# A recurrence between expert units: the x terms of four steps in one batch, the state product moved, VectorE's unit pass split over two gaps

## The reference

```python
logits = concatenate([x, h]) @ W_attn.T + b_attn        # 64 values
applied = softmax(logits) @ enc                          # enc: 64 x 128 of this sample
comb = relu(concatenate([x, applied]) @ W_comb.T + b_comb)
h = tanh(comb @ W_ih.T + b_ih + h @ W_hh.T + b_hh)
out = h @ W_out.T + b_out                                # 0 once a step with mean(x) == 0 came
```

## Time and profile before

| | us |
|---|---|
| Median of 3 runs | 1224.45 |
| Lowest, highest | 1223.15, 1224.51 |
| Profiled execution, its own time | 1223.28 |
| Its span, first to last instruction | 1221.2 |
| PE busy in the span | 1055.8 (86%) |
| DVE, POOL, ACT busy | 742.1, 512.8, 429.8 |
| Mean granted TensorE clock, share of 2.4 GHz | 0.864 |

### The profile page before, as it was taken

How to read it: one execution, slowest core, us unless ns; L and a number is a source line. 1 busy time by engine, 2 the same in 40 slices (tenths; PEclk the granted TensorE clock), 3 DMA queues, 4 the chain that set the end, 5 groups by cost and what they waited for, 6 DMA issues and landing times. The chain is left out here.

```text
span 1221.2 us, 31046 instructions
## 1 busy us (share of the span) xinstructions
PE 1055.8 (86%) x12668; PEld 701.2 (57%) x12668; DVE 742.1 (61%) x1882; ACT 429.8 (35%) x798; POOL 512.8 (42%) x452
## 2 busy tenths in 40 slices
PE   2699777789998999989997997799899999997867
PEld 2577655545555555545553443677677677775445
DVE  5544444445567554765569565678777678775553
ACT  1211011112221221212221222677778677775111
POOL 4788200003322332322333455576666666664010
PEclk9555555559999998889999999799999999999878
DMA  9020026012212221113222342000000000000000
GB/s 241 19 57 1 1 43 121 1 47 63 70 53 54 74 70 54 53 36 74 70 70 70 90 121 70 1 3 3 3 3 2 3 3 3 2 3 3 1 18 17
DMA packets 46066, 51.67 MB, mean 42 GB/s; under 512 B 22086, under 2 KB 36584, under 8 KB 45928
## 3 DMA queue, kind: packets, MB, share of 16 engines
q1 hardware_dynamic: 43010, 48.71, 15.7%
q10 hardware_dynamic: 2918, 1.01, 0.5%
HBM read 48.13 MB, written 1.57 MB: 41 GB/s over the span
## 5 line engine op out<-in xcount | busy, mean ns | idle before, releaser
L637 POOL TENSOR_TENSOR ex<-ex,xn 128x512 f32<-128x512 f32 x128 | 162.5, 1271 | 368.0 <-DVE ex L1173 275.3
L801 ACT ACTIVATE thcb<-ps 128x512 f32<-128x512 f32 x132 | 78.6, 596 | 283.1 <-PE ps L1529 283.1
L702 POOL TENSOR_TENSOR wu<-encC,wu 128x1024 f16<-128x1024 f32 x64 | 137.7, 2167 | 56.5 <-ACT encC L876 56.5
L1168 DVE SCALAR_TENSOR_TENSOR ex<-thcb,ps 128x512 f32<-128x512 f32 x132 | 90.6, 687 | 89.8 <-ACT thcb L801 87.1
L1536 PE MATMUL ps<-ex,wd 128*128 128x512 f32 x256 | 138.9, 625 | 1.9 <-POOL ex L637 1.9
L1529 PE MATMUL ps<-xnT,wg 128*128 (+1 forms) x384 | 109.3, 395 | 6.5 <-DVE ex L1173 6.4
L1529 PE MATMUL ps<-xnT,wu 128*128 (+1 forms) x384 | 109.7, 396 | 0.0
L1589 PE MATMUL ps<-wg,M 128*128 128x128 f16 x1536 | 98.2, 222 | 2.1 <-DVE wg L1262 2.1
L1589 PEld LDWEIGHTS ps<-wg,M 128*128 128x128 f16 x1536 | 93.1, 99 | 6.8 <-DVE wg L1262 2.5
L1173 DVE TENSOR_TENSOR ex<-ex,ps 128x512 f32<-128x512 f32 x132 | 90.7, 687 | 7.3 <-POOL ex L637 2.8
L696 POOL TENSOR_TENSOR wd<-wd,a_sum 128x512 f32<-128x512 f32 x64 | 66.5, 1042 | 65.7 <-DVE a_sum L1293 65.7
(11 more groups left out here) (295 smaller groups left out, 1937.1 us busy)
## 6 DMA issues: line engine op xcount, KB each, us to landing
xn<-coef_rows SPq DMA_DIRECT2D x128, 256.0 KB, 3.8
thcb<-in_L_ffn_Wg SPq DMA_DIRECT2D x8, 256.0 KB, 3.8
thcb<-in_L_ffn_Wu SPq DMA_DIRECT2D x8, 256.0 KB, 3.1
wd<-in_L_ffn_Wd SPq DMA_DIRECT2D x2, 1024.0 KB, 11.4
xtok<-in_x SPq DMA_DIRECT2D x4, 256.0 KB, 6.0
thcb<-in_ctx SPq DMA_DIRECT2D x2, 512.0 KB, 11.1
wu<-in_L_xcond_attn_wq SPq DMA_DIRECT2D x2, 512.0 KB, 10.9
wu<-in_L_xcond_attn_wk SPq DMA_DIRECT2D x2, 512.0 KB, 10.6
```

The source lines that it names most:

```text
L637: nc.gpsimd.tensor_tensor(hid[:, n % 2, :], gu[:, n % 2, :], other, ALU.mult)\
L702: nc.gpsimd.tensor_tensor(z[:, 1, 8 * u:8 * u + 8, :], a_Zc[:, u], z[:, 0, 8 * u:8 * u + 8, :], ALU.subtract)\
L801: nc.scalar.activation(th[:, n % 2, :], bank(n % 2), ACT.Tanh, scale=0.5 / WSCALE)\
L1168: V.scalar_tensor_tensor(ga[:, :], th[:, n % 2, :], 1.0, bank(n % 2), add, mul)\
```

## The change

Six things.

- The recurrence has two banks in every stage, 6 and 4. Bank 6 (`X_BANK`) holds, for four steps at once, comb (128 columns, 32 for each step) and the logits (partitions 32 times the step's number in its four); bank 4 (`Y_BANK`) the transposed exp and `hn`. `e_sb`, `nmax`, `esum`, `rsum` and `diag` use the same 32 partitions as the step's logits.
- `x_parts`: W_comb's x part, the logits' x part and the bias row of four steps, three matmuls of 128 columns, behind `hn` of every fourth step (and ahead of the first). The step itself has none of them. `xnc` and its copy are gone.
- The W_hh product comes right behind the 48 in every stage, and the 48 begin on the high half of `eb` alone.
- VectorE's unit is split: `gated` (first pass) one gap after TensorE's, `product` (second pass) two gaps after, ahead of all but the recurrence in its gap.
- Sides alternate over all units (`side`), also from chunk to chunk, and everything waits for the unit before the last. The shared unit has a gap of its own, one later; `END_GAP` goes from 96 to 97 and with it the sum into xT to gap 33.
- The loop over stages 2 and 3 is written out.

```diff
@@ -153,11 +152,11 @@
...
-        e_sb = sb("e_sb", [B, 2 * L])
-        nmax = sb("nmax", [B, 1])
-        esum = sb("esum", [B, 1])
-        rsum = sb("rsum", [B, 1])
-        diag = sb("diag", [B, B])
+        e_sb = sb("e_sb", [P, 2 * L])
+        nmax = sb("nmax", [P, 1])
+        esum = sb("esum", [P, 1])
+        rsum = sb("rsum", [P, 1])
+        diag = sb("diag", [P, B])
         eb = sb("eb", [P, 2, B], F16)
@@ -310,16 +309,19 @@
...
-        def step_banks(k):
-            return (7, 6, 5, 4) if first(k) else (6, 6, 6, 6)
+        X_BANK, Y_BANK = 6, 4
...
-        COMB, ET, HN = (slice(2 * L + i * B, 2 * L + (i + 1) * B) for i in range(3))
+        ET, HN = slice(0, B), slice(B, 2 * B)
+        LOGITS = slice(TL * B, TL * B + 2 * L)
+        def rows(st):
+            return slice(st % TL * B, (st % TL + 1) * B)
@@ -437,7 +439,7 @@
...
         U0 = 28
-        unit_gap = [U0 + 2 * min(n, PAIRS - 1) for n in range(UNITS)]
+        unit_gap = [U0 + 2 * n - (n == PAIRS) for n in range(UNITS)]
         END_GAP = unit_gap[-1] + 6
@@ -447,17 +449,19 @@
...
-            if isinstance(m, int) and m == 0 and n < 2:
-                return None
-            return m * UNITS + n - (1 if n else 0)
+            done = m * UNITS + n
+            return done - 1 if done >= 2 else None
+        def side(m, n):
+            return (m * UNITS + n) % 2
...
             stage(1, 0, None, True)
-            with eng.Fori(0, CH - 2) as j:
-                stage(j + 2, j + 1, j, True)
+            for k in range(2, CH):
+                stage(k, k - 1, k - 2, True)
             stage(CH, CH - 1, CH - 2, False)
@@ -634,7 +638,7 @@
...
                 other = wide if n < PAIRS else k_shared.broadcast_to([P, CT])
-                nc.gpsimd.tensor_tensor(hid[:, n % 2, :], gu[:, n % 2, :], other, ALU.mult)\
+                nc.gpsimd.tensor_tensor(hid[:, side(m, n), :], gu[:, side(m, n), :], other, ALU.mult)\
                   .then_inc(s["hid_ready"], 1)
@@ -762,20 +766,15 @@
...
                 act.wait_ge(s["nmax_ready"], t + 1)
-                nc.scalar.activation(e_sb[:, :], bank(step_banks(k)[0])[0:B, 0:2 * L], ACT.Exp, bias=nmax[:, :],
-                                     accum_out=esum[:, :]).then_inc(s["exp_ready"], 1)
+                r = rows(st)
+                nc.scalar.activation(e_sb[r, :], bank(X_BANK)[r, LOGITS], ACT.Exp, bias=nmax[r, :],
+                                     accum_out=esum[r, :]).then_inc(s["exp_ready"], 1)
...
                 act.wait_ge(s["hn_ready"], t + 1)
-                nc.scalar.activation(Hc[:, st, :], bank(step_banks(k)[3])[:, HN], ACT.Tanh, bias=bh[:, :])\
+                nc.scalar.activation(Hc[:, st, :], bank(Y_BANK)[:, HN], ACT.Tanh, bias=bh[:, :])\
                   .then_inc(s["h_ready"], 1)
-            def xn_chunk(k):
-                if not first(k):
-                    act.wait_ge(s["hn_ready"], k * SPC)
-                nc.scalar.copy(xnc[:, :], xnT[:, bass.ds(k * CT, CT)]).then_inc(s["xnc_ready"], 1)
@@ -798,12 +797,10 @@
...
                     act.wait_ge(s["gu_ready"], others(m, n))
-                nc.scalar.activation(th[:, n % 2, :], bank(n % 2), ACT.Tanh, scale=0.5 / WSCALE)\
+                nc.scalar.activation(th[:, side(m, n), :], bank(side(m, n)), ACT.Tanh, scale=0.5 / WSCALE)\
                   .then_inc(s["th_ready"], 1)
             def stage(k, m, tail, recur):
-                if recur:
-                    xn_chunk(k)
                 for gap in gaps_of(m, tail):
@@ -1014,28 +1011,28 @@
...
                 t = k * SPC + st
-                logits_bank, comb_bank, eT_bank, _ = (bank(i) for i in step_banks(k))
+                x_bank, eT, r = bank(X_BANK), bank(Y_BANK)[:, ET], rows(st)
                 if place == 0:
                     dve.wait_ge(s["logits_ready"], t + 1)
-                    V.tensor_reduce(nmax[:, :], logits_bank[0:B, 0:L], AX_X, ALU.max, negate=True)\
+                    V.tensor_reduce(nmax[r, :], x_bank[r, LOGITS.start:LOGITS.start + L], AX_X, ALU.max, negate=True)\
                      .then_inc(s["nmax_ready"], 1)
...
                     dve.wait_ge(s["exp_ready"], t + 1)
-                    rt.settle(V.reciprocal(rsum[:, :], esum[:, :]))
-                    V.tensor_scalar(diag[:, :], ident[0:B, 0:B], rsum[:, :], 2.0, mul, mul)\
+                    rt.settle(V.reciprocal(rsum[r, :], esum[r, :]))
+                    V.tensor_scalar(diag[r, :], ident[r, r], rsum[r, :], 2.0, mul, mul)\
                      .then_inc(s["diag_ready"], 1)
...
-                    V.tensor_tensor(eb[:, 0, :], eT_bank[:, ET], ebmask[:, :], mul).then_inc(s["eb_hi"], 1)
+                    V.tensor_tensor(eb[:, 0, :], eT, ebmask[:, :], mul).then_inc(s["eb_hi"], 1)
                     dve.wait_ge(s["eb_hi"], t + 1)
                     for a in range(2):
-                        r = slice(a * L, (a + 1) * L)
-                        V.tensor_tensor(eb[r, 1, a::2], eT_bank[r, ET][:, a::2], eb[r, 0, a::2], sub)\
+                        half = slice(a * L, (a + 1) * L)
+                        V.tensor_tensor(eb[half, 1, a::2], eT[half, a::2], eb[half, 0, a::2], sub)\
                          .then_inc(s["eb_lo"], 1)
...
                     dve.wait_ge(s["comb_ps_ready"], t + 1)
-                    V.tensor_scalar(comb[:, :], comb_bank[:, COMB], bcomb[:, :], 0.0, add, ALU.max)\
+                    V.tensor_scalar(comb[:, :], x_bank[:, rows(st)], bcomb[:, :], 0.0, add, ALU.max)\
                      .then_inc(s["comb_ready"], 1)
@@ -1160,17 +1157,20 @@
...
-            def unit(m, n):
+            def gated(m, n):
                 done = m * UNITS + n
                 dve.wait_ge(s["th_ready"], done + 1)
-                if others(m, n) is not None or n == 1:
+                if done:
                     dve.wait_ge(s["gu_ready"], done)
-                V.scalar_tensor_tensor(ga[:, :], th[:, n % 2, :], 1.0, bank(n % 2), add, mul)\
+                V.scalar_tensor_tensor(ga[:, :], th[:, side(m, n), :], 1.0, bank(side(m, n)), add, mul)\
                  .then_inc(s["unit_dve"], 1)
+            def product(m, n):
+                done = m * UNITS + n
                 dve.wait_ge(s["unit_dve"], done + 1)
...
                     dve.wait_ge(s["hid_ready"], others(m, n))
-                V.tensor_tensor(gu[:, n % 2, :], ga[:, :], bank(2 + n % 2), mul).then_inc(s["gu_ready"], 1)
+                V.tensor_tensor(gu[:, side(m, n), :], ga[:, :], bank(2 + side(m, n)), mul).then_inc(s["gu_ready"], 1)
@@ -1188,6 +1188,8 @@
...
                         rnn(k, st, place)
+                    for chunk, n in units_at(gap, m, tail, 2):
+                        product(chunk, n)
                     if first(k) and gap in SPLITS:
@@ -1202,7 +1204,7 @@
...
                     for chunk, n in units_at(gap, m, tail, 1):
-                        unit(chunk, n)
+                        gated(chunk, n)
@@ -1437,53 +1439,43 @@
...
+            def x_parts(t):
+                xs, x_bank = xnT[:, t * B:(t + TL) * B], bank(X_BANK)
+                mm(x_bank[:, 0:TL * B], w_T[:, 0, :], xs, start=True, stop=False, skip_group_check=True)
+                mm(x_bank[:, LOGITS], xs, w_attnT[:, 0, :], start=False, stop=False, skip_group_check=True)
+                mm(x_bank[:, LOGITS], ones_row[:, :], battn_row[:, :], start=False, stop=False, skip_group_check=True)
             def rnn(chunk, st, place):
...
                 h_prev = Hc[:, (st - 1) % SPC, :]
-                xs = xnc[:, st * B:(st + 1) * B]
-                lb, cb, tb, hb = (bank(i) for i in step_banks(chunk))
-                logits, comb_ps, eT, hn = lb[0:B, 0:2 * L], cb[:, COMB], tb[:, ET], hb[:, HN]
-                ahead = first(chunk)
-                def logits_of_x(st):
-                    mm(logits, xnc[:, st * B:(st + 1) * B], w_attnT[:, 0, :], start=True, stop=False)
-                    mm(logits, ones_row[0:1, 0:B], battn_row[:, :], start=False, stop=False)
+                x_bank, r = bank(X_BANK), rows(st)
+                logits, comb_ps = x_bank[r, LOGITS], x_bank[:, r]
+                eT, hn = bank(Y_BANK)[:, ET], bank(Y_BANK)[:, HN]
                 if place == 0:
-                    if st == 0:
-                        pe.wait_ge(s["xnc_ready"], chunk + 1)
-                        if ahead:
-                            logits_of_x(st)
+                    if t == 0:
+                        x_parts(0)
                     pe.wait_ge(s["h_ready"], t + 1)
-                    if not ahead:
-                        logits_of_x(st)
-                    mm(logits, h_prev, w_attnT[:, 1, :], start=False, stop=True).then_inc(s["logits_ready"], 1)
+                    mm(logits, h_prev, w_attnT[:, 1, :], start=False, stop=True, skip_group_check=True)\
+                        .then_inc(s["logits_ready"], 1)
                 elif place == 1:
                     pe.wait_ge(s["diag_ready"], t + 1)
```

(23 more changed lines are left out.)

## The result

| | us |
|---|---|
| Kernel before, median on this chip (range) | 1223.8 (1221.72 to 1224.51) |
| Changed kernel, median of 4 runs (range) | 1245.15 (1235.86 to 1245.43) |
| Ratio, 95% interval | 1.0159 (1.0110 to 1.0208) |
| Profiled execution: span, PE busy, DVE busy | 1243.7, 1037.0, 772.3 |

What follows compares the result with a forecast made beforehand. TensorE's matmul queue was taken as the bound in undisturbed full-clock steps, the softmax chain at half clock without units. Terms summed to -33.8 us, the clock -4, total -37.8: 1186 us forecast, range 1168 to 1206.

Steps and rivals of the forecast that it cites:

- VectorE's second pass one gap later: Full-clock recurrence step: reciprocal about 0.2 late, diag transpose 0.1 late, +0.12 us a step, bounds 0 and +0.69.
- Rival C: VectorE becomes the bound: second pass costs its full 0.69 ahead of the reciprocal in 40 steps, +23, 1209 us; chance 0.07.
- The queue is the bound, what leaves it is time: Undisturbed full-clock step: TensorE's matmul queue bounds, softmax chain about 0.1 us ahead; removing x and bias gives -0.80.
- steps of 7.5 or more: Sign in the profile after: undisturbed steps this long, in us, would refute that the queue is the bound.
- Undisturbed steps of 7.05, every fourth 8.3: Sign in the profile after: recurrence step lengths in us, where undisturbed steps took 7.74 before.
- The batch: Every fourth step, three products of 128 columns behind hn: 1.25 us at full clock, 1.6 counted at half clock.
- Stages at 140, 122.5, 134.5 and 141: Forecast lengths in us of recurrence stages 0 to 3, where these were 143.5, 138.8, 139.7 and 153.1.
- Total 1186: Forecast median in us of the whole changed kernel, from a total change of -37.8; chance 0.48.
- Loop written out, sides, later sum: -1.5 together: Loop's end and a copy of x -1.9, alternating buffers -1.0, later sum into xT +1.4 us.
- later sum: Sum into xT behind eb: down product stalls 1.9 where about 1.2 was lost before, +0.7 in each of two stages.
- The clock, -4: Half-clock stretches of stage 3: -4 of 11.7 us, as the first stretch probably goes; bounds -11.7 and +12.
- rival E: Slower than before by the clock alone, decided once 80 more us are at half clock; 1238 with 110 more; chance 0.06.

Runs made afterwards that it cites:

- e9: Changed kernel with VectorE's second unit pass yet another gap later, behind diag (last two units of a chunk excepted), identity in SBUF: 1204.00 us, ratio to before 0.9857.
- e1: Changed kernel with only diag's identity read from a 32x32 place in PSUM, filled by one matmul: 1191.32 us, ratio to the kernel before 0.9758.
- e2: Changed kernel with VectorE's second unit pass put back in the gap of its first: 1217.39 us, ratio to the kernel before 0.9969.
- e6: Changed kernel with diag's identity in PSUM and both VectorE passes in one gap: 1205.97 us, ratio to the kernel before 0.9865.
- e4: Changed kernel with the old recurrence and both VectorE passes in one gap; shared unit's gap, sides and written-out loop stay: 1231.11 us, ratio to before 1.0074.
- e5: Kernel before with only diag's identity moved to PSUM: 1214.52 us, ratio to the kernel before 0.9938.
- e7: Changed kernel with three extra bf16 matmuls, results unread, ahead of the wait for diag in stages 1 to 3: 1239.59 us, ratio to before 1.0158.
- e3: Changed kernel with the old recurrence (x terms and bias in every step), second pass still one gap later: 1281.66 us, ratio to the kernel before 1.0502.

## Why the prediction was wrong

- **VectorE's second pass one gap later: +0.12, bounds 0 and +0.69.** This step failed. What it priced was right: e9, where the pass isn't ahead of the reciprocal, has (29.32 - 28.79) / 4 = 0.13 us less a step than e1. What it left out was what the pass releases: GpSimd's unit, which then lies over diag and holds it, +0.9 in each of 36 steps beside units, 33 us. The upper bound asked only whether the pass would be held up by GpSimd, and no other VectorE instruction was asked about. Of the rest of the error of 59 us, 8 are e1's own distance from the forecast (0.9758 of 1223.8 is 1194) and some 10 or more the clock; the remainder isn't assigned.
- **Rival C** named the right pair of engines and dismissed it with "GpSimd waits for VectorE, not the reverse". That sentence read semaphores. The hold shows in no wait of VectorE's: only in diag's duration, which in the kernel before ran from 0.23 to 1.3 us for one 32x32 form.
- **The queue is the bound, what leaves it is time.** Right only as long as the chain keeps up. In e9 the transpose has no idle time ahead of it, and the step takes 6.93 us, 0.81 less than 7.74: the 0.80 forecast, whole. In e1 TensorE stands idle 0.1 there, as forecast, and the step is 7.11. With the passes together the same 0.8 us out of the queue brought 0.04 (e2), and TensorE stands idle 0.69 for diag. So steps of 7.5 or more, which were to refute the statement, came in e2 (7.70) and e6 (7.53), where VectorE's two passes make the chain the bound. Timeline of e9, an undisturbed step (the 0.42 of the weight load is there in the kernel before too):

```profile
589.50 0.23 DVE L1023 TENSOR_SCALAR diag<-ident,rsum 32x32 f32<-32x32 f32 x1
589.86 0.29 PEld L1464 LDWEIGHTS ps<-diag,e_sb 32*128 32x128 f32 x2 [0.42 <-DVE diag L1023]
589.86 0.40 PE L1464 MATMUL ps<-diag,e_sb 32*128 32x32 f32 x2
```

- **Undisturbed steps of 7.05, every fourth 8.3.** e1 has 7.11 to 7.22 and 7.86; the four take 29.32 for 29.45 forecast. The batch cost 0.75 in its step and 0.1 in the next, not 1.25.
- **Stages at 140, 122.5, 134.5 and 141.** e1: 139.3, 123.5, 139.0 and 139.5. **Total 1186** (the sum as written, 1185.5 and 1.2, is 1186.7): e1 1191, by ratio 30 of the 38 us forecast. The sum was near for a kernel without the hold, in part by errors that cancel: stage 2 came out 4.5 over, with 17 us of half clock where none was forecast, and stage 3 1.5 under.
- **Loop written out, sides, later sum: -1.5 together.** e4 says +0.7% (9 us), with the loop's end itself shorter by 4.5; in e1 and the changed kernel the step across it is 11.2 us for 17.29, without its 10.2 us of half clock. Not settled which part costs. For the later sum, the stall was right and what it replaces was not: e1's down product waits 1.91 us for xT (1.9 forecast), but the sum's old place cost 0.43 (e5) and not 1.2, so +1.5 a stage and not +0.7. Timeline of e1:

```profile
393.55 1.47 PE L1530 MATMUL ps<-ex,wd 128*128 128x512 f32 x2 [1.91 <-DVE xT L1180]
```

- **The clock, -4, and rival E.** It went the other way: 90.7 us of half clock between tanh 16 and 63 before, 135.7 after. That is 45 more, short of the 80 from which E was to decide, and e7 took most of it away with no gain that the runs can tell. The kernel is slower as E had it, but not by the clock alone: e1 keeps the thinner queue and is 2.4% faster than before.

## What to carry to other kernels

Before moving an instruction on VectorE, lay the GpSimd instructions that it releases over VectorE's own list, and ask of every VectorE instruction under them whether it reads and writes SBUF alone; diag and the four scalings of xn2c did, and were held, and a small constant kept in PSUM was a cheap way out for diag. Look for one form with two durations in the profile before: its longest is what each of them may cost once the order shifts. And when a queue is made shorter, check what engine the next instruction of the chain stands behind, since the gain may need a second edit, as here.

## What the runs showed of the hardware

- A 32x32 scaling from SBUF to SBUF that starts 0.03 us after a GpSimd product of 128x512 ends with it (1.27 us for 0.24); with the source in PSUM it isn't held at all. Nor is the first pass, whose second input lies in PSUM: in e9 it runs right under GpSimd's unit and takes its usual 0.69. Timeline of e9:

```profile
577.84 1.27 POOL L641 TENSOR_TENSOR ex<-ex,xn 128x512 f32<-128x512 f32 x1 [4.97 <-DVE ex L1173]
577.87 0.69 DVE L1165 SCALAR_TENSOR_TENSOR ex<-thcb,ps 128x512 f32<-128x512 f32 x1
```

- One and the same wait of 0.87 us left the clock full in the undisturbed steps of e3's stage 1 (8.68 us a step) and went with 3.4 to 3.6 us of half clock in each undisturbed step of stages 2 and 3 (10.25 to 10.46). What decides between the two isn't shown.
- Three bf16 matmuls of 384 columns took 0.65 us at full clock.
